# FFN with conditioning on one core: other SBUF places for TensorE's operands, and other zero products at the start

## The reference

```
h    = gelu(einsum('btel,elf->btef', x, W1) + b1)        # per group: 128 -> 512
y    = einsum('btef,efl->btel', h, W2) + b2              # per group: 512 -> 128
eo   = silu(cond) @ emb_W + emb_b                        # 4 rows, 1024 -> 2048
hn   = layernorm(y, ln_g, ln_b) * (1 + scale) + shift    # scale, shift: halves of eo
out  = x + silu(hn) @ out_W + out_b                      # 1024 -> 1024
```

## Time and profile before

| | |
|---|---|
| median of 3 runs | 714.31 us (714.11 to 714.84) |
| profiled execution, its own time | 714.53 us |
| span of the profiled execution, first to last instruction | 712.3 us |
| PE busy | 708.5 us, 3166 products |
| PEld (weight loads) busy | 581.9 us, 3166 loads |
| DVE busy | 523.6 us |
| ACT busy | 451.1 us |
| POOL busy | 96.0 us |

### The profile page before, as it was taken

One profiled execution on the slowest core, in us unless ns is written; L12 is line 12 of the kernel. 1 busy time (PEld: TensorE's weight loads), 2 busy tenths in 40 slices (PEclk: granted clock), 3 DMA queues, 4 the chain that ended last, 5 costly groups with the idle time before them and its releaser, 6 DMA issues.

```text
span 712.3 us, 8201 instructions
## 1 busy us (share of the span) xinstructions
PE 708.5 (99%) x3166; PEld 581.9 (82%) x3166; DVE 523.6 (74%) x555; ACT 451.1 (63%) x494; POOL 96.0 (13%) x69
## 2 busy tenths in 40 slices
PE   9999999999999999999999999999999999999998
PEld 6888885888888888888888888888888888888887
DVE  6887885888777779889966868767678676687511
ACT  7787784778787788898872665554455454555500
POOL 0000000000000010200112332231322322322100
PEclk9999999999999999999999999999999999999999
DMA  5567572564413713323169767667566676565531
GB/s 180 175 240 263 195 250 89 180 117 152 149 63 114 266 60 119 100 77 119 50 229 282 218 195 192 180 190 224 178 202 170 186 222 195 189 177 137 160 118 60
DMA packets 55607, 118.62 MB, mean 167 GB/s; under 512 B 11904, under 2 KB 32896, under 8 KB 52496
## 3 DMA queue, kind: packets, MB, share of 16 engines
q1 hardware_dynamic: 42608, 101.22, 40.8%
q0 software_dynamic: 4608, 16.78, 12.1%
q10 hardware_dynamic: 8352, 0.10, 0.7%
HBM read 67.72 MB, written 33.59 MB: 142 GB/s over the span
## 4 chain that ended last, share of the span: by engine, by line
PE 99%; DVE 0%; issue 0%; POOL 0%; POOLq 0%
PE psum L820 47%; PE psum L798 24%; PE psum L782 24%; PE psum L876 2%; PE psum L809 1%; PE psum L828 1%; PE psum L842 0%; DVE res L760 0%; POOL zeros L342 0%; POOLq L916 0%
## 5 line engine op out<-in xcount | busy, mean ns | idle before, releaser
L573 DVE TENSOR_TENSOR g_lo<-g_raw,g_hi 128x1024 fp32r<-128x1024 f32 x128 | 158.3, 1237 | 61.3 <-ACT g_hi L409 58.7
L403 ACT ACTIVATE g_raw<-psum,cols 128x1024 f32<-128x1024 f32 x127 | 141.7, 1116 | 57.2 <-PE psum L782 48.8
L820 PE MATMUL psum<-oW_lo,s_hi 128*128 128x512 f32 x496 | 152.9, 389 | 0.0
L820 PE MATMUL psum<-oW_hi,s_lo 128*128 128x512 f32 x496 | 152.8, 389 | 0.0
L820 PE MATMUL psum<-oW_hi,s_hi 128*128 128x512 f32 x496 | 152.8, 389 | 0.0
L798 PE MATMUL psum<-g_hi,W 128*128 128x512 f32 x512 | 136.9, 389 | 0.0
L782 PE MATMUL psum<-xT_hi,W 128*128 128x512 f32 x508 | 136.1, 390 | 0.0
L798 PEld LDWEIGHTS psum<-g_hi,W 128*128 128x128 f32 x512 | 96.1, 188 | 20.0
L782 PEld LDWEIGHTS psum<-xT_hi,W 128*128 128x128 f32 x508 | 95.2, 188 | 20.8 <-issue 0.8
L733 DVE TENSOR_TENSOR res<-psum,res 128x1024 f32<-128x1024 f32 x31 | 38.0, 1224 | 98.9 <-PE psum L820 92.3
L820 PEld LDWEIGHTS psum<-oW_hi,s_lo 128*128 128x128 f32 x496 | 93.1, 188 | 19.3
(11 more groups left out here) (74 smaller groups left out, 588.6 us busy)
## 6 DMA issues: line engine op xcount, KB each, us to landing
y_scratch<-y_stage SPq DMA_DIRECT2D x32, 512.0 KB, 3.0
yb<-y_scratch SPq DMA_DIRECT2D x16, 1024.0 KB, 4.8
res<-in_x SPq DMA_DIRECT2D x32, 512.0 KB, 6.2
res<-out_b_all POOLq DMA_DIRECT2D x32, 512.0 KB, 4.5
xT_raw<-in_xT SPq DMA_DIRECT2D x31, 512.0 KB, 4.5
out<-res SPq DMA_DIRECT2D x31, 512.0 KB, 3.9
emb_raw<-in_emb_W SPq DMA_DIRECT2D x8, 1024.0 KB, 7.6
wraw<-in_out_W SPq DMA_DIRECT2D x16, 256.0 KB, 4.9
```

Of the source, the lines that this page charges most:

```text
L403: nc.scalar.activation(g_raw[:, m % 2], ring(m), ACT.Gelu, bias=cols[:, R_B1 + k:R_B1 + k + 1]).then_inc(gelu_done, 1)
L573: nc.vector.tensor_tensor(g_lo[:, m % 2], g_raw[:, m % 2], g_hi[:, m % 2].bitcast(F32), ALU.subtract).then_inc(glo_done, 1)
L820: mm = nc.tensor.matmul(proj(q)[:, half], v[:, g, cut], w[:, g, half], start=(g == 0 and k == 0), stop=(g == G - 1 and k == 2))
```

## The change

Three things. (1) The moving operands of stage A and the stationary operands of stage B move by less than 512 bytes: modulo 512 bytes xT_hi lies at 32, xT_lo at 64, g_hi at 128, g_lo at 256, s_lo0 at 96, s_hi0 at 192, s_hi1 at 320, s_lo1 at 448. W, oW_hi and oW_lo stay at 0. Neighbours (g_raw, y_stage, yb1, sq, out_b_all, mean_part1, three emb_raw) move so that nothing overlaps. (2) The tile `zeros`, its memset and its semaphore go. The zero products now read a constant of one column, repeated with step 0, and are two of 512 columns instead of two of 512 and one of 128. (3) In `first(1)` the parts are made in the order hi x hi, hi x lo of x, lo of W x hi, so that the wait for `w_split` stands before the last part.

```diff
-        zeros = at("zeros", [P, P], S0 + 8704)
-        emb_raw = [at(f"emb_raw{k}", [P, 2 * D], R0 + o * KB) for k, o in enumerate((0, 104, 112, 120))]
+        emb_raw = [at(f"emb_raw{k}", [P, 2 * D], R0 + o * KB + (512 if o else 0)) for k, o in enumerate((0, 104, 112, 120))]
-        xT_hi = at("xT_hi", [P, 2, TA], R0 + 56 * KB, F32R)
-        xT_lo = at("xT_lo", [P, 2, TA], R0 + 64 * KB, F32R)
-        g_raw = at("g_raw", [P, 2, TA], R0 + 72 * KB)
-        g_hi = at("g_hi", [P, 2, TA], R0 + 80 * KB, F32R)
-        g_lo = at("g_lo", [P, 2, TA], R0 + 88 * KB, F32R)
-        y_stage = at("y_stage", [P, 2, TA], R0 + 96 * KB)
+        xT_hi = at("xT_hi", [P, 2, TA], R0 + 56 * KB + 32, F32R)
+        xT_lo = at("xT_lo", [P, 2, TA], R0 + 64 * KB + 64, F32R)
+        g_raw = at("g_raw", [P, 2, TA], R0 + 72 * KB + 64)
+        g_hi = at("g_hi", [P, 2, TA], R0 + 80 * KB + 128, F32R)
+        g_lo = at("g_lo", [P, 2, TA], R0 + 88 * KB + 256, F32R)
+        y_stage = at("y_stage", [P, 2, TA], R0 + 96 * KB + 256)
-        s_lo0 = at("s_lo0", [P, G, TP], R0 + 8 * KB, F32R)
-        s_hi1 = at("s_hi1", [P, G, TP], R0 + 16 * KB, F32R)
-        s_lo1 = at("s_lo1", [P, G, TP], R0 + 24 * KB, F32R)
+        s_lo0 = at("s_lo0", [P, G, TP], R0 + 8 * KB + 96, F32R)
+        s_hi1 = at("s_hi1", [P, G, TP], R0 + 16 * KB + 320, F32R)
+        s_lo1 = at("s_lo1", [P, G, TP], R0 + 24 * KB + 448, F32R)
...
-        s_hi0 = at("s_hi0", [P, G, TP], R0 + 124 * KB, F32R)
+        s_hi0 = at("s_hi0", [P, G, TP], R0 + 124 * KB + 704, F32R)
...
-            nc.gpsimd.memset(zeros[:], 0.0).then_inc(zeros_set, 1)
...
-                for k, (w, v) in enumerate(((W1_HI, xT_hi), (W1_LO, xT_hi), (W1_HI, xT_lo))):
-                    if m == 1 and k == 1:
+                parts = [(W1_HI, xT_hi), (W1_LO, xT_hi), (W1_HI, xT_lo)]
+                if m == 1:
+                    parts = [parts[0], parts[2], parts[1]]
+                for k, (w, v) in enumerate(parts):
+                    if m == 1 and k == 2:
                         pe.wait_ge(w_split, 1)
...
-            pe.wait_ge(zeros_set, 1)
-            for parts in (4, 4, 1):
-                nc.tensor.matmul(psum[:, 7, 0:parts * P], zeros[:], zeros[:].unsqueeze(1).to_broadcast([P, parts, P]),
+            zero = nc.const_aps.tensor(0.0, [P, 1], F32)
+            for j in range(2):
+                nc.tensor.matmul(psum[:, 7], zero.to_broadcast([P, P]), zero.to_broadcast([P, BANK]),
                                  start=True, stop=True)
```

More of the change, by code:

```diff
@@ L120, in cond_ffn_program @@
         xT_raw = at("xT_raw", [P, 2, TA], R0 + 48 * KB)
-        xT_hi = at("xT_hi", [P, 2, TA], R0 + 56 * KB, F32R)
-        xT_lo = at("xT_lo", [P, 2, TA], R0 + 64 * KB, F32R)
-        g_raw = at("g_raw", [P, 2, TA], R0 + 72 * KB)
-        g_hi = at("g_hi", [P, 2, TA], R0 + 80 * KB, F32R)
-        g_lo = at("g_lo", [P, 2, TA], R0 + 88 * KB, F32R)
-        y_stage = at("y_stage", [P, 2, TA], R0 + 96 * KB)
+        xT_hi = at("xT_hi", [P, 2, TA], R0 + 56 * KB + 32, F32R)
[4 more added lines that the diff above has]
+        y_stage = at("y_stage", [P, 2, TA], R0 + 96 * KB + 256)
         yb0 = at("yb0", [P, G, TP], R0)
         tanh0 = at("tanh0", [P, G, TP], R0 + 8 * KB)
-        s_lo0 = at("s_lo0", [P, G, TP], R0 + 8 * KB, F32R)
-        s_hi1 = at("s_hi1", [P, G, TP], R0 + 16 * KB, F32R)
-        s_lo1 = at("s_lo1", [P, G, TP], R0 + 24 * KB, F32R)
+        s_lo0 = at("s_lo0", [P, G, TP], R0 + 8 * KB + 96, F32R)
+        s_hi1 = at("s_hi1", [P, G, TP], R0 + 16 * KB + 320, F32R)
+        s_lo1 = at("s_lo1", [P, G, TP], R0 + 24 * KB + 448, F32R)
         res = at("res", [P, 4, D], R0 + 48 * KB)
         yb2 = at("yb2", [P, G, TP], R0 + 64 * KB)
-        yb1 = at("yb1", [P, G, TP], R0 + 104 * KB)
-        sq = at("sq", [P, G, TP], R0 + 112 * KB)
-        out_b_all = at("out_b_all", [P, D], R0 + 120 * KB)
-        s_hi0 = at("s_hi0", [P, G, TP], R0 + 124 * KB, F32R)
-        mean_part1 = at("mean_part1", [P, HG, TP], R0 + 124 * KB)
+        yb1 = at("yb1", [P, G, TP], R0 + 104 * KB + 512)
+        sq = at("sq", [P, G, TP], R0 + 112 * KB + 512)
+        out_b_all = at("out_b_all", [P, D], R0 + 120 * KB + 512)
+        s_hi0 = at("s_hi0", [P, G, TP], R0 + 124 * KB + 704, F32R)
+        mean_part1 = at("mean_part1", [P, HG, TP], R0 + 124 * KB + 512)
         yb = (yb0, yb1, yb2)
@@ L143, in cond_ffn_program @@
         W1_HI, W1_LO, W2_HI, W2_LO = range(4)
-        zeros_set = sem("zeros_set")
         eps_set = sem("eps_set")
```

## The result

The kernel after takes 728.64 us (median of 4 runs, 728.36 to 729.09), the kernel before 714.58 us (4 runs, 714.11 to 714.84). The ratio is 1.0199, 95% interval 1.0187 to 1.0212: 2% slower, 14.1 us. The forecast was 714.1 us with a range of 692 to 722. The profiled execution has a span of 726.4 us, 14.1 us more than before, so the profile shows all of it.

A forecast was written before the change was run, and what follows sets the result against it. PE, busy 100% between head and tail, was taken as the bound. From the median 714.31 us, 0.23 us for the head and 0 for the eight places came off, giving 714.1 us, range 692 to 722.

The forecast's parts named there:

- part 1: The eight new places in FFN and projection: claimed worth zero, between 33 us gain and 41 us loss.
- the row that varies the place: Embedding products (L809), stationary place moving in 128-byte steps: passes stay 0.43 us apart, so place has no effect.
- the caveat: Embedding loads have 32 columns, not 128, with remainder 0.0025 us instead of 0.0133; used to bound the gain.
- The second reason for zero: FFN and projection: same remainder at 256 and 512 columns, DVE at 98% or 58%; a collision would be expected to vary.
- the remainder: Time in each FFN and projection product that no column accounts for: 0.0133 us, 41 us over 3096 products.
- rival (a): FFN and projection: remainder is interference of load and stream, another place removes it; 681.0 us, chance 0.11.
- Rival (c): FFN and projection slower: xT_hi and s_lo0 start at odd multiples of 32 bytes, 10.3 us, 724.4 us; chance 0.11.
- the bound of 41 us upwards: FFN and projection: all 3096 products pay the remainder once more for reads starting off a 512 byte line.
- The head: Kernel start: zero products without POOL wait, first real product 0.40 us earlier, first(1) and the end 0.23 us earlier.
- the upper bound (8.3 us): Head: a gap of 0.28 us after the zero products delays the clock's rise to 8.3 us, costing 1.2 us.
- rival (d): Head: the clock rises later still, at 10 us, losing 2.2 us, 716.3 us; chance 0.02.
- The costs of DVE's and ACT's work at nothing: Other engines' accesses to moved tiles: no row shows place matters, DVE's cast stays at 687 ns, cost nothing.

The follow-up runs named there:

- e3: Kernel before with everything in SBUF, weights too, moved by 32 bytes, relative places unchanged: 714.85 us, ratio 1.0006.
- e7: Kernel before with stage A's moving operands and stage B's weights all at place 64: 728.07 us, ratio 1.0190.
- e6: Kernel before with stage A's moving operands at place 128 and stage B's weights at 32: 733.12 us, ratio 1.0259.
- e9: Kernel before with stage A's moving operands and stage B's weights at place 192: 731.1 us, single runs from 728.06 to 734.40.
- e17: Kernel before, all places 0, each product's weights replaced by one repeated column (output not the reference's): 725.15 us, ratio 1.0137.
- e18: Repeated weight column as in e17, with the places of e5 (stage A at 32, stage B's weights at 128): 728.85 us, ratio 1.0202.
- e5: Kernel before with stage A's moving operands at place 32 and stage B's weights at 128: 734.79 us, ratio 1.0281.
- e15: Kernel before with only the low parts moved by 128 modulo 256 (xT_lo, g_lo, s_lo): 729.95 us, ratio 1.0214.
- e4: Kernel before with all shifted operands (stage A moving, stage B weights) at one place, 256: 714.38 us, ratio 1.0000.
- e12: Kernel before with stage A's moving operands at place 160 and stage B's weights at 96, difference +160 in both: 737.52 us, ratio 1.0327.
- e14: Kernel before with moving operands 4 bytes (one word) off the weights' place in both stages: 739.71 us, ratio 1.0351.
- e11: Kernel before with stage A's moving operands at place 96 and stage B's weights at 160, difference +96 in both: 735.10 us, ratio 1.0288.

## Why the prediction was wrong

**The step that failed** is in part 1: "Between ends this far apart I take zero, because the row that varies the place is the one that has no effect". All 14.1 us are there; the places cost 0.0044 us a product in stage A and 0.0052 in stage B where I had 0. The embedding did vary the place, and still shows no effect: in the profile after its rows are 0.43 us apart as in the earlier trace rows. But it is another kind of product. Its pass takes 0.429 us for 512 columns, two cycles of 2.4 GHz a column, and its loads are 32 columns, so it needn't say anything of a stream at one column a cycle beside a load of 128. Which of these hides the effect was not tested. I had named the caveat for the size of the gain and then used the row as if it held for the sign.

**The second reason for zero**, that the remainder is the same in both stages, at two widths and beside a busy or a less busy DVE, was true and proved less than I took from it. In all those rows the difference of places was the same, 0 modulo 256. A remainder that depends on that difference alone must be constant there. (the earlier trace rows are too short to show it, since 45 products in 10 us are good to 2%; the starts of single products there give 0.2267.) The one variable in question did not vary in any row but the embedding's.

**The point for rival (a)** was right as an observation and wrong in its direction. The remainder does depend on the places, for most of them by 16 cycles, but before it was at its lowest: none of the seven other multiples of 32 is better than 0, and the least bad costs 0.0023 us.

**Rival (c)** had the sign, a chance of 0.11 and the wrong mechanism. It charged a start at an odd multiple of 32 bytes, 0.0133 us for 772 products, 724.4 us. e3 moves both operands to such a start for nothing; e7, e6 and e9 charge 64, 128 and 192 as well, which are even multiples. Each of the seven multiples of 32 between 0 and 256 costs, 0.0023 to 0.0077 us a product, and most of the 3096 products lie at one of them. I had written down the bound of 41 us upwards and then closed the range at 722.

**The Trainium skill**, "SBUF — State Buffer", section "Who interferes with whom", says that PE and ACT never wait on anyone, and "TensorE: Matmul & The Clock Gate", section "Step-by-step: what each phase is for", cited in the prediction, that loading the next weights takes no read bandwidth from the running product. These runs agree for DVE beside PE: 0.2267 us holds with DVE 58% or 98% busy. They disagree for PE with itself: e17 against before, and e18 against e5, change nothing but what the load reads and change the distance by +0.0046 and -0.0019 us on the mean of the two stages. The prediction said that by the rule this part is worth nothing, and that this trace neither proves nor breaks it; the measurement decides against it.

**The head** came nearly as forecast: 0.20 us earlier at `first(1)` in the trace against 0.23, through the same steps (load at 0.73, ACT's cast as the new bound, the rise of the clock that takes back a part). The sizes were less good, and partly made up for each other. The first real product stood at 4.84 us before and not at 4.98, so it gained 0.29 us and not 0.40, and the clock took back 0.10 and not 0.17. The new order of `first(1)` had nothing to hide in this execution: DVE's low part of W was ready at 6.29 us, before a load of 6.64 could want it. The later rises of the clock that the upper bound (8.3 us) and rival (d) (10 us) took stand in no row; here the products were 0.23 us apart from 5.48 us on, as before from 5.68 on. The row of before, with its first real product:

```profile
4.84 1.47 PE L842 MATMUL psum<-xT_hi,W 128*128 128x512 f32 x4
```

The costs of DVE's and ACT's work at nothing were right too: the cast that I had priced at 687 ns has a mean of 689:

```profile
L568 DVE CAST g_hi<-g_raw 128x1024 fp32r<-128x1024 f32 x65 | 44.8, 689 | 1.3 <-ACT g_raw L400 0.7 <-PE psum L799 0.6
```

**What stays open.** Why the price of one difference takes two values (+64: 0.2290 or 0.2333) and why a few products at another place make those at place 0 dear (e15). Both look like a phase that one product hands to the next, and that the distances of e6 and e17 change at the embedding and stay changed fits it; no run was made to test it. Why 16 bytes cost in one stage and not in the other. And what the 0.0133 us at place 0 are made of: no run got under them for 512 columns.

## What to carry to other kernels

When PE is busy all the time, divide a long stretch by the number of weight loads in it; a change of a few ns in that quotient is microseconds at the end, and no wait will show it. For fp32r products of 512 columns with a load of 128 each, as here, keep the moving operand and the weights at the same place modulo 256 bytes (offsets that are multiples of 256 do it), and treat a shift "to spread the addresses" as a change that needs its own run. A row that is to stand in for a missing one must have the same rates, not only the same variable.

## What the runs showed of the hardware that I had not expected

- The distance of two 512 column products depends on the difference of the two operands' places: 0.2267 us at 0 and 256, 0.2290 to 0.2344 us at the seven multiples of 32 between them (e4 to e12), 0.2368 at 4 bytes (e14, stage A). Moving both operands by 32 bytes changes nothing (e3).
- With 256 columns the order is another one. By the starts of the 48 pieces it is 0.1198 us with the weights at 0 (before), 0.1134 at the places of the change and with all weights at 64 (e7), 0.1185 at 128 (e5) and 0.1200 at 160 (e11).
- The same program can run at two speeds at a granted clock of 1.00: 728.1 and 734.2 us (e9), 722.4 and 727.9 us (e17). That the distance of the products is the reason is inferred, from a change of it inside one execution (e6: 0.2333 us before the embedding, 0.2324 behind it).
